# Vision tower kernel, one core: both image halves are loaded before the embedding matrix, and all patch strips are turned before the embedding begins

## The chip, the cores and the metric

One core of a Trainium2 chip runs the whole kernel in float32. The metric is the device time in microseconds (us), as the median of several executions. The profile is of one execution. Its engines are PE (TensorE matmul; PEld is its weight load), DVE (VectorE), ACT (ScalarE), POOL (GpSimd) and SP (SyncE, which here only issues transfers).

## The reference, cut to what matters

Sixteen images of 96 x 96 x 3 are cut into 6 x 6 patches of 16 x 16 x 3 = 768 values. Each patch is multiplied by a 768 x 192 matrix (the embedding), and attention and a soft mixture of 64 small MLPs follow.

```
h = einsum('bnk,kd->bnd', extract_patches(x, 16), W_proj) + b_proj + pos_emb   # 16 x 36 x 192
h = h + attention(layernorm(h))                    # 12 heads of 16, 36 tokens per image
h = h + soft_moe(layernorm(h))                     # 64 slots, fc1 192x768, gelu, fc2 768x192 each
```

The 64 pairs of fc1 and fc2 matrices are 75.5 MB of the 79.74 MB that the core moves. The change is in the first line alone.

## The kernel before

**Tiles.** There are 576 tokens. They are held in six row tiles `t` of three images (108 tokens), the last of one image (36 tokens). A patch's 768 values are six chunks of 128, which are the contraction of the embedding. Chunks 0 to 2 come from the upper eight pixel rows of each patch (`ph` = 0), chunks 3 to 5 from the lower eight (`ph` = 1).

**Images to chunks.** SP loads one half (`ph`) of all images with one DMA of 864 KB into `x_rows`: 96 partitions, one for each image and patch row, each 8 pixel rows long. Each half goes through the same steps:

1. `pixels` (L229) reorders the pixels so that each of the six patch columns `nw` is contiguous. DVE does columns 0 and 1 and then 2 and 3 (L633, two copies), ACT does columns 4 and 5 (L440, one copy).
2. PE turns each strip `n` = 6 ph + nw with three transposes of 96 x 128 (L907) into one of four PSUM banks (`n % 4`). It waits at L901 or L903 for the reordered pixels, and at L905 until the strip four before it has been copied out.
3. ACT copies the even strips to `patchesT` (L443), DVE the odd ones (L636). Both count them, in `x_kept_a` and `x_kept_d`, up to three for a half.

DVE and ACT work in program order, so the reordering of the second half stands behind the copies of the first half's strips on both engines.

**Embedding.** `embed(t, chunks)` (L877) issues one matmul per chunk (L881), with 192 columns out, into bank `4 + t % 4`. Tiles 0 to 3 keep their banks until their six chunks are summed, tiles 4 and 5 reuse banks 4 and 5. In the trace a float32 matmul or transpose is two records, so one strip of three transposes is six records and `embed(t, range(3))` is six records.

**Order on PE before the change.** Nine filler matmuls (`keep_busy`, L875, whose result nothing reads), then strips 0 to 5; two fillers; a wait for the matrix (`wp_in`) and for the six kept strips; `embed` of tiles 0 and 1 with chunks 0 to 2; strips 6 to 11; `embed` of tiles 2 and 3 with chunks 0 to 2; a wait for all twelve kept strips; and from L1092 on chunks 3 to 5 of tiles 0 to 2, the turning of the attention weights (`turn_weights`) between the rest of the embedding, and layer norm, attention and the routing.

**Order on SP.** First half of the images, embedding matrix, second half, three copies of the positional table, the biases and attention weights, and then the MLP's weights in units of 1536 KB (L270). The ring has room for 12 units. The last six slots overlap the buffers of the embedding and of the attention weights, so SP waits at L275 and L276 before it fills them. The other 36 units each wait at L281 until PE has used the unit in their slot, which first happens when the MLP begins. PE works through 48 units in eight groups of six.

```
x_in[ph]   -> DVE L633, ACT L440         (reordering)
wp_in      -> PE, ahead of the first embed
embedded   -> DVE L642 (adds the positional table, then layer norm), SP L275
```

Of the kernel before, what the change touches and what calls it, by code (L numbers as in the profile page):

```python
# [11 lines left out]
def vit_tower_kernel(nc, x, tok_w, tok_b, tok_pos, w_qkv, w_proj, attn_b, slots, slot_scale,  # L12
# [9 lines left out]


    B, IMG, _, CH = x.shape
    KP, D = tok_w.shape
    N = tok_pos.shape[0]
    GRID = 6
    PATCH = IMG // GRID
    NT = B * N
    HEADS, DH = 12, 16  # L30
    S, _, FF = fc1_w.shape
    EPS = 1e-5
    TPI = 3
# [23 lines left out]
    def rows(t):  # L57
        return min(TR, NT - TR * t)
# [4 lines left out]
    with ExitStack() as ctx:  # L63
# [3 lines left out]
        def sem(name):  # L67
            return ctx.enter_context(nc.semaphore(name))
# [101 lines left out]
        wqkv_in, wproj_in, wp_in = sem("wqkv_in"), sem("wproj_in"), sem("wp_in")  # L170
# [10 lines left out]
        x_turned, x_kept_a, x_kept_d = sem("x_turned"), sem("x_kept_a"), sem("x_kept_d")  # L181
# [60 lines left out]
        @block.sync  # L242
        def _(sp):
            for ph in range(2):
                sp.dma_start(x_rows[0:C2, ph, :],
                             x_view[:, ph * 8 * XR:(ph + 1) * 8 * XR]).then_inc(x_in[ph], 16)
                if ph == 0:
                    sp.dma_start(embed_w[:, :, :], tok_w.rearrange("(c p) d -> p c d", p=128)).then_inc(wp_in, 16)
            for j in range(TPI):
                sp.dma_start(pos_raw[j * N:(j + 1) * N, :], tok_pos).then_inc(pos_in, 16)  # L250
            sp.dma_start(pos_b[0:TR, :], tok_b.partition_broadcast(TR)).then_inc(pos_in, 16)
            sp.dma_start(qkv_raw[0:C2], w_qkv.rearrange("(t p) c -> p t c", p=C2)).then_inc(wqkv_in, 16)
            sp.dma_start(proj_raw[0:C2], w_proj.rearrange("(t p) c -> p t c", p=C2)).then_inc(wproj_in, 16)
            sp.dma_start(slot_rows[0:S, :], slots).then_inc(slots_in, 16)
            sp.dma_start(slot_sc[0:S, 1:2], slot_scale.rearrange("(s a) -> s a", a=1)).then_inc(slots_in, 16)
            sp.dma_start(b1_raw[0:S, :], fc1_b).then_inc(b1_in, 16)
            sp.dma_start(attn_b_row[0:TR, :], attn_b.partition_broadcast(TR)).then_inc(ab_in, 16)
            sp.dma_start(norm_row[0:TR, :], norm_w.partition_broadcast(TR)).then_inc(nw_in, 16)
            sp.dma_start(b2_rows[0:S, :], fc2_b).then_inc(b2_in, 16)

            def load_unit(g, slot):
                u = slot % UNITS
                if u < 3:
                    dst = ring[:, slot, :].rearrange("p (q o) -> p q o", q=GS // 2)
                    src = fc1_view[u][:, bass.ds(g * (GS // 2), GS // 2), :]
                else:
                    dst = ring[:, slot, :].rearrange("p (s n) -> p s n", s=GS)
                    src = fc2_view[:, bass.ds(g * GS, GS), 2 * (u - 3):2 * (u - 3) + 2, :].rearrange(
                        "p s c d -> p s (c d)")
                sp.dma_start(dst, src).then_inc(unit_in[slot], 16)  # L270

            for slot in range(RING):
                if slot == EARLY:

                    sp.wait_ge(embedded, TT)  # L275
                    sp.wait_ge(misc_turned, 2)  # L276
                load_unit(slot // UNITS, slot)
            with sp.Fori(1, GROUPS // 2) as it:
                for slot in range(RING):

                    sp.wait_ge(units_used, it * RING + (slot + 1 - RING))  # L281
                    load_unit(it * 2 + slot // UNITS, slot)
            for tt in range(3):
                sp.wait_ge(final_ready, (1, 2, 4)[tt])
                if tt < 2:
                    sp.dma_start(out_view[2 * tt * TR:2 * (tt + 1) * TR, :].rearrange("(t p) d -> p t d", p=TR),
                                 h[0:TR, 2 * tt:2 * tt + 2, :]).then_inc(out_written, 16)
                else:
                    for t in (TT - 2, TT - 1):
                        sp.dma_start(out_view[t * TR:t * TR + rows(t), :],  # L290
                                     h[0:rows(t), t, :]).then_inc(out_written, 16)
            sp.wait_ge(out_written, 64)
# [577 lines left out]
        def _(pe):  # L870
            def keep_busy(bank, count):


                for _ in range(count):
                    pe.matmul(ps[:, bank, 0:128], ident[:, :], ident[:, :], start=True, stop=True)  # L875

            def embed(t, chunks=range(KC)):  # L877
                if t >= 4:
                    pe.wait_ge(h_ready, t - 3)
                for c in chunks:  # L880
                    mm = pe.matmul(ps[0:rows(t), 4 + t % 4, 0:D], patchesT[:, c, t * TR:t * TR + rows(t)],  # L881
                                   embed_w[:, c, :], start=(c == 0), stop=(c == KC - 1))
                if chunks[-1] == KC - 1:
                    mm.then_inc(embedded, 1)
# [4 lines left out]
            for n in range(2 * GRID):  # L889
                if n == 6:  # L890

                    keep_busy(7, 2)
                    pe.wait_ge(wp_in, 16)
                    pe.wait_ge(x_kept_a, 3)
                    pe.wait_ge(x_kept_d, 3)
                    for t in range(2):
                        embed(t, range(3))
                ph, nw = n // 6, n % 6

                if nw < 4:  # L900
                    pe.wait_ge(regrouped_d, 2 * ph + nw // 2 + 1)  # L901
                else:
                    pe.wait_ge(regrouped_a, ph + 1)  # L903
                if n >= 4:
                    pe.wait_ge(x_kept_d if n % 2 else x_kept_a, (n - 4) // 2 + 1)  # L905
                for r in range(3):
                    mm = pe.transpose(ps[:, n % 4, r * C2:(r + 1) * C2],  # L907
                                      x_patch[0:C2, ph, nw, r * 128:(r + 1) * 128], ident[0:C2, 0:C2])
                mm.then_inc(x_turned, 1)

            embed(2, range(3))
            embed(3, range(3))
            pe.wait_ge(x_kept_a, 6)
            pe.wait_ge(x_kept_d, 6)

# [385 lines left out]
```

## Time and profile before

| | us |
|---|---|
| median of 3 runs | 247.25 |
| the three runs | 245.79, 247.25, 251.49 |
| span of the profiled execution, first to last instruction | 244.4 |
| PE busy in the span | 221.5 (91%) |
| DVE, ACT, POOL busy | 67.4, 64.0, 44.2 |
| data moved | 79.74 MB, mean 326 GB/s |

The profiled execution's own device time is not shown apart from its span; the median of the runs is 2.85 us above that span, the fastest run 1.39 us. The span is cut into 40 slices of 6.1 us on the page. The images, the strips and the embedding fill the first four or so, attention and routing go to about 85 us, and the MLP's eight groups take the rest. A busy share says only that an engine was at work: which wait ends last in a stretch is read from the chain and the timelines.

### The profile page before, as it was taken

To read this page: it belongs to the slowest core of one execution; us is meant where nothing else is said; L and a number is where in the kernel's file an instruction comes from. 1 tells how busy PE (TensorE), PEld (TensorE's weight loads), DVE (VectorE), ACT (ScalarE), POOL (GpSimd) and SP (SyncE) were. 2 spreads that over 40 slices of the span, in tenths; PEclk is the share of its full clock that TensorE was granted. 3 is DMA by queue.
4 is the path that set the end of the run, shared out by engine and by line. 5 is a ranking of instruction groups with operands and counts; after the bars stand their busy time and mean duration, and the time that the engine had idled before them with its cause. 6 is when DMAs were issued, how large, how long until landed. Compare 5 with 4: busy or idle time off the path is not lost.

```text
span 244.4 us, 5457 instructions
## 1 busy us (share of the span) xinstructions
PE 221.5 (91%) x2268; PEld 157.2 (64%) x2268; DVE 67.4 (28%) x166; ACT 64.0 (26%) x160; POOL 44.2 (18%) x80
## 2 busy tenths in 40 slices
PE   6799999999998889978979979997997999799794
PEld 6789756777767737635548547764664675576472
DVE  0557346678766532011011002002000200200202
ACT  2443242454656734021021021003002100300300
POOL 7501268663534020000000000001000000000000
PEclk9999999999999999997999997997699999999999
DMA  6999999999800059999999999999999999999952
GB/s 164 266 240 400 393 373 380 398 394 373 306 1 3 0 174 409 388 373 384 400 387 373 385 402 388 374 385 402 388 373 386 401 388 373 385 402 387 373 208 72
DMA packets 40904, 79.74 MB, mean 326 GB/s; under 512 B 1096, under 2 KB 28344, under 8 KB 40696
## 3 DMA queue, kind: packets, MB, share of 16 engines
q1 hardware_dynamic: 40888, 79.52, 90.8%
q8 instruction: 11, 0.18, 0.3%
q14 instruction: 5, 0.04, 0.0%
HBM read 79.07 MB, written 0.44 MB: 325 GB/s over the span
## 4 chain that ended last, share of the span: by engine, by line
PE 70%; DMA 9%; SPq 8%; ACT 5%; issue 3%; DVE 3%; POOL 1%; DVEq 0%; ACTq 0%
PE ps L1263 12%; PE ps L1223 11%; PE ps L875 10%; SPq L270 8%; DMA ring<-in_L_ffn_fc_weight_dram 6%; PE ps L1203 6%; PE ps L881 5%; PE ps L995 4%; PE ps L950 3%; DMA ring<-in_x_dram 3%; ACT region_p L593 2%; PE ps L968 2%; PE ps L1193 2%; PE ps L1239 2%; PE ps L907 2%
## 5 line engine op out<-in xcount | busy, mean ns | idle before, releaser
L875 PEld LDWEIGHTS ps<-ident 128*128 128x128 f32 x310 | 40.3, 208 | 10.6 <-issue 8.6
L875 PE MATMUL ps<-ident 128*128 128x128 f32 x310 | 44.9, 301 | 1.8 <-POOL neg_half L307 1.8
L846 DVE TENSOR_TENSOR region_p<-ps,b1T 128x384 f32<-128x384 f32 x16 | 8.2, 553 | 124.0 <-PE ps L1239 124.0
L1263 PE MATMUL ps<-ring,region_p 128*32 128x192 f32 x768 | 37.8, 352 | 1.2 <-ACT region_p L608 0.9
L1263 PEld LDWEIGHTS ps<-ring,region_p 128*32 128x32 f32 x768 | 24.9, 119 | 11.7 <-ACT region_p L608 2.7
L1223 PE MATMUL ps<-ring,qkvT 128*32 128x384 f32 x288 | 26.8, 490 | 0.0
L593 ACT COPY region_p<-ps 128x384 f32<-128x384 f32 x16 | 11.7, 831 | 55.3 <-PE ps L1223 55.3
L1203 PE MATMUL ps<-region_k,soft_space 128*108 128x192 f32 (+1 forms) x96 | 18.6, 336 | 0.4 <-ACT region_k L610 0.4
L1203 PEld LDWEIGHTS ps<-region_k,soft_space 128*108 128x108 f32 (+1 forms) x96 | 13.7, 163 | 7.1 <-issue 6.3
L429 POOL COPY qkvT<-region_k 128x384 f32 x6 | 3.1, 513 | 79.8 <-PE ps L1223 79.8
L1239 PE MATMUL ps<-ident,region_p 128*128 128x128 f32 x48 | 7.0, 282 | 11.4 <-ACT region_p L593 11.4
L610 ACT COPY region_k<-ps 128x192 f32<-128x192 f32 x8 | 2.5, 318 | 54.0 <-PE ps L1263 54.0
L352 POOL TENSOR_TENSOR region_k<-region_k,head_mask 96x432 f32<-96x432 f32 x16 | 14.3, 910 | 9.0 <-PE ps L968 6.8
L1239 PEld LDWEIGHTS ps<-ident,region_p 128*128 128x128 f32 x48 | 5.1, 141 | 16.3 <-ACT region_p L593 16.3
L1223 PEld LDWEIGHTS ps<-ring,qkvT 128*32 128x32 f32 x288 | 8.1, 109 | 9.9 <-issue 8.8
L881 PE MATMUL ps<-ring 128*108 128x192 f32 (+1 forms) x72 | 12.6, 328 | 0.1
L995 PE MATMUL ps<-qkvT,soft_space 96*108 96x192 f32 x64 | 11.8, 328 | 0.0
L608 ACT ACTIVATE region_p<-region_p 128x384 f32<-128x384 f32 x16 | 7.5, 514 | 15.4 <-DVE region_p L846 15.4
L881 PEld LDWEIGHTS ps<-ring 128*108 128x108 f32 (+1 forms) x72 | 10.8, 163 | 0.9 <-issue 0.2
L1193 PE MATMUL ps<-v_diag,region_k 64*128 64x288 f32 x32 | 10.5, 451 | 0.0
L995 PEld LDWEIGHTS ps<-qkvT,soft_space 96*108 96x108 f32 x64 | 10.2, 173 | 0.3 <-ACT soft_space L469 0.2
L1223 PE MATMUL ps<-ring,region_k 128*32 128x384 f32 x96 | 8.5, 489 | 0.6 <-DVE region_k L825 0.6
(137 smaller groups left out, 235.1 us busy)
## 6 DMA issues: line engine op xcount, KB each, us to landing
ring<-in_L_ffn_fc_weight_dram SPq DMA_DIRECT2D x48, 1536.0 KB, 15.9
ring<-in_x_dram SPq DMA_DIRECT2D x2, 864.0 KB, 8.8
ring<-in_L_tok_W_proj_dram SPq DMA_DIRECT2D x1, 576.0 KB, 7.7
ring<-in_L_attn_w_qkv_dram SPq DMA_DIRECT2D x1, 432.0 KB, 11.2
out_dram<-h SPq DMA_DIRECT2D x2, 162.0 KB
ring<-in_L_ffn_fc_bias_dram SPq DMA_DIRECT2D x1, 192.0 KB, 9.5
ring<-in_L_attn_w_proj_dram SPq DMA_DIRECT2D x1, 144.0 KB, 11.7
soft_space<-in_L_tok_pos_emb_dram SPq DMA_DIRECT2D x3, 27.0 KB
```

Source lines behind the costliest of these rows:

```text
L270: sp.dma_start(dst, src).then_inc(unit_in[slot], 16)
L352: pool.tensor_tensor(k_diag[0:C2, i % 2, og, :].rearrange("p (a h m) -> p a h m", a=2, h=HG), kT[0:C2, og, 2 * N * i:2 * N * (i + 1)].rear ...
L593: act.copy(hid[:, :, half * 64:(half + 1) * 64].rearrange("p c n -> p n c"), ps[:, half, 0:FF // 2].rearrange("p (n c) -> p n c", c=FC)).t ...
L846: dve.tensor_tensor(pre[:, 3 * half:3 * half + 3, :].rearrange("p c (s b) -> p c s b", s=GS), ps[:, 2 + half, 0:384].rearrange("p (c s b) ...
L875: pe.matmul(ps[:, bank, 0:128], ident[:, :], ident[:, :], start=True, stop=True)
L881: mm = pe.matmul(ps[0:rows(t), 4 + t % 4, 0:D], patchesT[:, c, t * TR:t * TR + rows(t)], embed_w[:, c, :], start=(c == 0), stop=(c == KC - 1))
L995: mm = pe.matmul(ps[0:TR, 2 + i % 2, a * D:(a + 1) * D], x_copies[0:C2, i % 2, c, a, :], qkvT[0:C2, c, 2 * D:3 * D], start=(c == 0), stop= ...
L1193: mm = pe.matmul(ps[:, half, 0:HALF], sel[0:S, gg, :], combT[0:S, half * HALF:(half + 1) * HALF], start=True, stop=True)
L1203: mm = pe.matmul(ps[0:r, 5 + t // 2, (t % 2) * D:(t % 2 + 1) * D], mix[:, gg, t * TR:t * TR + r], y2[:, gg, :], start=False, stop=False, s ...
L1223: mm = pe.matmul(ps[32 * q:32 * q + 32, half, 0:FF // 2], y, w[:, q, half * FF // 2:(half + 1) * FF // 2], start=(j == 0), stop=(j == 2), ...
L1239: mm = pe.transpose(ps[:, 2 + c // 3, (c % 3) * 128:(c % 3 + 1) * 128], hid[:, c, :], ident[:, :])
L1263: mm = pe.matmul(ps[32 * q:32 * q + 32, 4, 0:D], gact[:, 2 * u + cc, 2 * q + l, :], w[:, 2 * q + l, cc, :], start=first, stop=last, tile_p ...
```

## The change

SP issues the embedding matrix after the second half of the images. On PE the embedding of tiles 0 and 1 between the halves is gone; four filler matmuls stand there and no wait. After strip 11, PE waits for the matrix and for the first half's kept strips, and then runs chunks 0 to 2 of tiles 0 to 3 in one block.

```diff
             for ph in range(2):
                 sp.dma_start(x_rows[0:C2, ph, :],
                              x_view[:, ph * 8 * XR:(ph + 1) * 8 * XR]).then_inc(x_in[ph], 16)
-                if ph == 0:
+                if ph == 1:
                     sp.dma_start(embed_w[:, :, :], tok_w.rearrange("(c p) d -> p c d", p=128)).then_inc(wp_in, 16)
...
             for n in range(2 * GRID):
                 if n == 6:
 
-                    keep_busy(7, 2)
-                    pe.wait_ge(wp_in, 16)
-                    pe.wait_ge(x_kept_a, 3)
-                    pe.wait_ge(x_kept_d, 3)
-                    for t in range(2):
-                        embed(t, range(3))
+                    keep_busy(7, 4)
                 ph, nw = n // 6, n % 6
...
-            embed(2, range(3))
-            embed(3, range(3))
+            pe.wait_ge(wp_in, 16)
+            pe.wait_ge(x_kept_a, 3)
+            pe.wait_ge(x_kept_d, 3)
+            for t in range(4):
+                embed(t, range(3))
             pe.wait_ge(x_kept_a, 6)
             pe.wait_ge(x_kept_d, 6)
```

## Rows read from the trace of the kernel before

**Rows 1.** Page, 40 slices of the span: DMA busy share in tenths, and GB/s.

```profile
DMA  6999999999800059999999999999999999999952
GB/s 164 266 240 400 393 373 380 398 394 373 306 1 3 0 174 409 388 373 384 400 387 373 385 402 388 374 385 402 388 373 386 401 388 373 385 402 387 373 208 72
```

**Rows 2.** Busy time by stretch: PE, PEld, DVE, ACT, POOL, granted clock, DMA share, GB/s.

```profile
20.00:60.00 40.00, 39.25 (x324) 29.14 (x323) 25.00 (x67) 17.06 (x55) 21.33 (x31) 1.00 1.04 387
60.00:86.00 26.00, 24.01 (x255) 19.11 (x258) 17.19 (x52) 16.05 (x52) 9.26 (x14) 1.00 0.25 89
...
100.00:150.00 50.00, 44.28 (x479) 28.03 (x471) 5.24 (x9) 8.15 (x15) 2.37 (x6) 0.94 1.05 386
150.00:200.00 50.00, 46.80 (x543) 31.73 (x546) 3.50 (x6) 5.75 (x11) 1.58 (x4) 0.92 1.05 387
200.00:237.00 37.00, 33.76 (x376) 22.95 (x368) 3.44 (x6) 5.09 (x9) 0.00 (x0) 1.00 1.01 368
```

**Rows 3.** The chain that ended last, in time: start, us, what.

```profile
0.81 6.17 DMA ring<-in_x_dram
7.62 3.14 PE ps L907 x18
10.77 0.78 PE ps L875 x4
11.63 2.17 PE ps L881 x12
13.84 1.21 PE ps L907 x12
...
221.33 15.71 DMA ring<-in_L_ffn_fc_weight_dram
```

**Rows 4.** Timeline of DVE (first three rows) and ACT: start, us, instruction, idle before.

```profile
7.01 1.03 DVE L633 COPY ring<-ring 96x768 f32<-96x768 f32 x2 [7.01 <-DMA ring<-in_x_dram]
...
10.80 0.68 DVE L636 COPY ring<-ps 128x288 f32<-128x288 f32 x1 [0.28 <-PE ps L907]
13.23 1.02 DVE L633 COPY ring<-ring 96x768 f32<-96x768 f32 x2 [1.75 <-DMA ring<-in_x_dram]
...
10.32 0.67 ACT L443 COPY ring<-ps 128x288 f32<-128x288 f32 x1 [0.28 <-PE ps L907]
13.23 0.83 ACT L440 COPY ring<-ring 96x768 f32<-96x768 f32 x1 [2.23 <-DMA ring<-in_x_dram]
```

**Rows 5.** Timeline of PE: the fillers early and late, the second half's strips, the embedding.

```profile
1.76 4.21 PE L875 MATMUL ps<-ident 128*128 128x128 f32 x18 [1.76 <-POOL neg_half L307]
...
13.84 2.02 PE L907 MATMUL ps<-ident,ring 96*128 96x96 f32 x18
15.70 5.05 PE L881 MATMUL ps<-ring 128*108 128x192 f32 x30
...
79.64 1.60 PE L875 MATMUL ps<-ident 128*128 128x128 f32 x12
```

**Rows 6.** SP's issues: start and us of the issue.

```profile
0.81 0.41 SPq L245 DMA_DIRECT2D ring<-in_x_dram  x1
1.29 0.41 SPq L248 DMA_DIRECT2D ring<-in_L_tok_W_proj_dram  x1
1.75 0.53 SPq L245 DMA_DIRECT2D ring<-in_x_dram  x1
...
4.21 0.36 SPq L252 DMA_DIRECT2D ring<-in_L_attn_w_qkv_dram  x1
...
87.21 2.26 SPq L270 DMA_DIRECT2D ring<-in_L_ffn_fc_weight_dram  x2
```

**Rows 7.** Page, DMA issues: count, KB each, median us from issue to landing.

```profile
ring<-in_x_dram SPq DMA_DIRECT2D x2, 864.0 KB, 8.8
ring<-in_L_tok_W_proj_dram SPq DMA_DIRECT2D x1, 576.0 KB, 7.7
ring<-in_L_attn_w_qkv_dram SPq DMA_DIRECT2D x1, 432.0 KB, 11.2
```

## The prediction

> **What bounds the kernel now.** I read the slices of the page first, then the busy times by stretch, then the chain of waits over the first 20 us, and last the timelines of the engines there. In the slices, DMA is at nine tenths or more, near 390 GB/s, until about 61 us, nearly idle for the next three slices, and busy again to the end [rows 1]. The stretches say the same in numbers: a DMA share of 1.04 from 20 to 60 us, 0.25 from 60 to 86 us, and 1.05, 1.05 and 1.01 in the MLP [rows 2]. So there are two regimes. Up to the MLP PE sets the pace (39.25 of 40 us and 24.01 of 26 us busy), with the transfers ahead of it. From the first reload at 87.21 us [rows 6] the transfers set the pace, and the chain ends with 15.71 us of waiting for MLP weights [rows 3]. A reload waits until PE has used the unit in its slot. **A shift of the MLP's start therefore moves all 36 reloads and the end by the same amount**, and nothing in the MLP gives it back. The idle DMA between 61 and 80 us means that an earlier or later load of units in front of the MLP changes nothing.
>
> The changed stretch lies in PE's regime. The chain goes from the first image half (0.81 + 6.17 = 6.98 us) to strips 0 to 5 (7.62 to 10.76), fillers (to 11.55), the embedding of tiles 0 and 1 (11.63 to 13.80), and strips 6 to 11 from 13.84 [rows 3]. PE's gaps after 7.62 us are under 0.1 us each. So the removed embedding was not wasted time: it filled the wait for the second image half, whose reordering DVE and ACT begin at 13.23 us, after 1.75 and 2.23 us of idling for it [rows 4].
>
> **The transfers.** The landing times come from issue plus latency. First half: 6.98 us. Matrix: 1.29 + 7.7 = 8.99 us. The two halves average 8.8 us, so the second took 2 x 8.8 - 6.17 = 11.4 us from 1.75, which is 13.2 us [rows 6, 7] and agrees with DVE's start at 13.23. After the change the second half is issued at about 1.3 us, and the trace has no second-in-line transfer of that size. From both sides: at the pace at which the matrix landed behind the first half, 2.0 us for 576 KB, it lands 3.0 us after 6.98, at 10.0 us; at the pace of the second half behind the matrix, 4.2 us for 864 KB, at 11.2 us. I take 11, nearer to the row with its own size and row length. The matrix is then last of three with the same bytes in total, so I take 13.2 us. It could be as late as the attention matrix, three small tables further back in the queue: 4.21 + 11.2 = 15.4 us [rows 6, 7]. SP's three issues take 0.41, 0.41 and 0.53 us in either order, and the issues behind them don't move.
>
> **When strips 6 to 11 start.** Three things must be ready. DVE's reordering stands behind its copy of strip 5, which ends at 10.80 + 0.68 = 11.48 us [rows 4]; that is later than the landing, so DVE's order decides and not the transfer. From the start of the reordering to the first strip took 13.84 - 13.23 = 0.61 us: 12.09 us. The four extra filler records (two matmuls) cost 1.60/12 = 0.13 us each at the late rate or 4.21/18 = 0.23 us at the early one [rows 5], so the fillers end at 12.1 or 12.5 us. The first is free, hidden under DVE's reordering; the second costs 0.4 us. I take 12.09. ACT is free for its part at 10.99 us and needs 0.83 us [rows 4]: 11.8, earlier than DVE. **The strips move 1.75 us earlier.** They take 15.70 - 13.84 = 1.86 us [rows 5], which holds their waits for the copies by ACT and DVE, and end at 13.95 us.
>
> **The embedding.** Before, 12 records of chunks 0 to 2 were left at 15.70 us; at 5.05/30 = 0.168 us each [rows 5] they end at 17.72. After, 24 are left at 13.95: 4.04 us, to 17.99. The matrix (13.2) is there in time, the first half's strips were kept at 11.48, and the second half's are wanted only at 18. **Sum: 17.99 - 17.72 = +0.27 us.** In words: a block of 2.0 us was moved from before the strips to behind them; the strips move up by 1.75 us, because DVE isn't free any sooner. The rest of the program follows in the same order and shifts with it. DVE, which would have idled for the first summed tile in any case, has its copies done some 1.75 us sooner, and that is worth nothing. The profiled execution has a span of 244.4 us; with 2.85 us around it, which brings it to the median of the runs, the forecast is 247.5 us.
>
> **The clock.** The granted clock reads 1.00 over all rows up to 60 us [rows 2], that is the 2.4 GHz level, but durations differ: 18 records of strips took 3.14 us in the first half [rows 3] and 2.02 us in the second, and a filler 0.23 us early and 0.13 us late [rows 5]. I read the early ones as run at 1.2 GHz. The rise came while PE had worked without a pause from 7.62 us, nearly all of that on transposes.
>
> The Trainium skill, page "TensorE: Matmul & The Clock Gate", section "Part 4: PE-mode transpose", says that the full clock does not engage for transposes, since they don't count as PE being busy in the same way. By that rule the change would be harmful: it puts all strips close together, with only fillers between, and takes the ordinary matmuls out. This trace speaks against it, as the rise followed 3.14 us of transposes and 0.78 us of fillers.
>
> **Rivals.**
>
> *The second half lands no earlier* (the change doesn't do what it says). All three transfers are in flight together, so the order of issue may matter little. Then strips start at 13.84 as before, end at 15.70, and 24 records follow, to 19.74: +2.0 us, 249.3 us. PE idles some 1.7 us where it embedded before. It begins to cost when the half lands after 11.48 us, one for one. Against it: the matrix landed 4.2 us ahead of the half issued 0.46 us behind it, so order does count. Chance 0.10. This is my slower case.
>
> *The matrix is late.* PE then waits behind the strips, with everything queued behind. It decides from 13.95 us on; at 15.4 us it adds 1.5 us to the 0.27: 249.0 us. For it: the matrix has 768-byte rows and now shares the engines with small tables. Against it: the same bytes are ahead of it. Chance 0.10.
>
> *Strips 0 to 5 run at the full clock.* In an execution where the clock rises during the first fillers, they would take about 1.86 us instead of 3.14, and DVE would be free at about 10.2. The old kernel gains nothing from that, as it waits for the half until 13.2. The new one starts the second strips at 10.6 to 11.8 (landing plus 0.61) and ends them at 12.5 to 13.6; it embeds from 13.2 to 13.6 on and ends at 17.2 to 17.7: -0.5 to 0 us, 246.8 to 247.2 us. In the profiled execution it wasn't so. Chance 0.20.
>
> *The clock falls behind the strips.* If PE went back to 1.2 GHz for the block of 24 records, they would cost up to twice, +4.0 us: 251.5 us. This is what the rule of the skill's page would lead to. Against it: the pause ahead of the strips is 0.1 us or less. Chance 0.05.
>
> **How the numbers follow.** The forecast, +0.1 to +0.7 us, has 0.50. Beside the four rivals 0.05 is left for what the runs themselves do: the three before spread from 245.79 to 251.49, 2.3%, without any change. A median may well fall near the fastest, which gives the low end: 245.79 - 0.5, rounded down to 245.0. The high end takes in the first two rivals at 249.3 and half a microsecond of spread: 249.8. Only the fallen clock and spread lie outside. A difference of 2% is 4.9 us, about what a measurement of this kernel can tell from no change; no rival reaches it, so faster has 0.02, slower 0.04 and within 2% the rest.
>
> **What would show it.** Right: DVE's reordering of the second half starts at 11.48 us without idling for the transfer; first strip of the second half at about 12.1; an unbroken block of 24 embedding records from about 13.95; its end within 0.5 us of 17.7; the first reload near 87.5. Wrong: DVE or ACT idle for the images past 11.5 us (first rival), PE idle ahead of the block (second), embedding records over 0.2 us apart (clock). A change of more than 2 us at the first reload would make the sum wrong; one behind it, with the reload in place, would make the claim of the rigid shift wrong.

## The result, and the profile after

The changed kernel takes 247.78 us (median of 20 runs) against 246.72 us before (20 runs). The ratio is 1.0063 with a 95% interval of 1.0033 to 1.0093, which is a cost of 0.8 to 2.3 us: a small loss, but clear of zero. The ratio leaves slow executions out, and its cut falls unevenly here: six of the changed kernel's at 249.3 to 249.9 us are counted, five of the kernel before at 250.6 to 251.5 (and one at 1172.85) are not, and with those six left out too the ratio of the means would be 1.0031. The medians differ by 1.06 us. The forecast was 247.5 us, +0.27 us. In the profiled pair the span went from 244.4 to 245.7 us, and the first reload of an MLP unit from 87.21 to 88.40 us.

The chain of waits of the changed kernel over its first 22 us (start, us, what), which answers to [rows 3]:

```profile
0.82 6.54 DMA ring<-in_x_dram
...
7.38 0.57 DVE ring L633
...
7.99 3.14 PE ps L902 x18
11.13 1.76 PE ps L875 x8
12.89 2.19 PE ps L902 x18
15.09 6.84 PE ps L881 x42
```

PE does not pause from 7.99 us on, and the embedding is one block, as intended. Three terms differ from the sum. The first image half landed at 7.36 instead of 6.98 us. The fillers hold PE up to 12.89 us, against the 12.1 us at which the strips were forecast. And from the start of the second strips to the start of the embedding are 14.93 - 12.69 = 2.24 us in PE's timeline below, where 1.86 was taken over from before.

DVE, and under it ACT's reordering of the second half, in the changed kernel's timeline, against [rows 4]:

```profile
7.38 1.02 DVE L633 COPY ring<-ring 96x768 f32<-96x768 f32 x2 [7.38 <-DMA ring<-in_x_dram]
...
11.17 0.68 DVE L636 COPY ring<-ps 128x288 f32<-128x288 f32 x1 [0.29 <-PE ps L902]
11.69 1.01 DVE L633 COPY ring<-ring 96x768 f32<-96x768 f32 x2
13.82 1.98 DVE L636 COPY ring<-ps 128x288 f32<-128x288 f32 x3 [1.12 <-PE ps L902]
...
11.15 0.85 ACT L440 COPY ring<-ring 96x768 f32<-96x768 f32 x1
```

The second reordering follows the copy of strip 5 with no idle time for a transfer in its row. The prediction had this step, with the right releaser: the order of DVE's own program. DVE then waits 1.12 us for PE, which is still at its fillers.

PE's timeline and SP's issues (start, us), against [rows 5] and [rows 6], and the page's DMA rows (median us from issue to landing), against [rows 7]:

```profile
10.93 1.97 PE L875 MATMUL ps<-ident 128*128 128x128 f32 x8
12.69 2.40 PE L902 MATMUL ps<-ident,ring 96*128 96x96 f32 x18
14.93 7.00 PE L881 MATMUL ps<-ring 128*108 128x192 f32 x42
...
0.82 0.87 SPq L245 DMA_DIRECT2D ring<-in_x_dram  x2
1.73 0.42 SPq L248 DMA_DIRECT2D ring<-in_L_tok_W_proj_dram  x1
...
88.40 10.96 SPq L270 DMA_DIRECT2D ring<-in_L_ffn_fc_weight_dram  x4
...
ring<-in_x_dram SPq DMA_DIRECT2D x2, 864.0 KB, 7.8
ring<-in_L_tok_W_proj_dram SPq DMA_DIRECT2D x1, 576.0 KB, 10.7
```

The matrix lands at 1.73 + 10.7 = 12.4 us, ahead of the strips' end at 14.9. The two halves average 7.8 us and the first took 6.54, so the second took 9.1 us from about 1.27 and landed near 10.3. Both were needed later than that.

From the first reload to the end of the span are 157.2 us before and 157.3 us after. In this pair the MLP passes the shift on whole; its stretches have DMA shares of 1.05 and 1.05, as before [rows 2].

```profile
100.00:150.00 50.00, 44.25 (x530) 28.51 (x526) 5.19 (x9) 8.15 (x15) 2.38 (x6) 1.00 1.05 387
150.00:200.00 50.00, 46.83 (x528) 31.72 (x518) 3.56 (x6) 5.76 (x11) 1.58 (x4) 0.90 1.05 387
```

So the first reload of an MLP unit ("the reload" from here on) is a gauge of the front of the kernel that is free of what the long MLP adds. The experiments are read by it first, and then by their times.

### The profile page after: what moved, and what is told of

The parts are those of the page before. It is cut to its first block, busy times and chain, and to the rows that moved or that the text cites. A ratio compares the mean times of both kernels' runs of the same rounds, so it can differ in the third digit from the quotient of the medians.

```text
span 245.7 us, 5465 instructions
## 1 busy us (share of the span) xinstructions
PE 221.5 (90%) x2272; PEld 158.1 (64%) x2272; DVE 67.3 (27%) x166; ACT 64.0 (26%) x160; POOL 44.5 (18%) x80
## 4 chain that ended last, share of the span: by engine, by line
PE 61%; SPq 17%; DMA 9%; ACT 4%; issue 3%; DVE 3%; POOL 1%; DVEq 0%; ACTq 0%
SPq L270 17%; PE ps L1261 9%; PE ps L1221 9%; PE ps L875 8%; DMA ring<-in_L_ffn_fc_weight_dram 6%; PE ps L881 5%; PE ps L1201 5%; PE ps L993 4%; PE ps L948 3%; DMA ring<-in_x_dram 3%; PE ps L966 2%; PE ps L902 2%; ACT region_p L593 2%; PE ps L1237 2%; PE ps L1008 2%
## 5 line engine op out<-in xcount | busy, mean ns | idle before, releaser
L875 PEld LDWEIGHTS ps<-ident 128*128 128x128 f32 x314 | 41.2, 210 | 10.7 <-issue 8.7
L875 PE MATMUL ps<-ident 128*128 128x128 f32 x314 | 45.9, 302 | 1.8 <-POOL neg_half L307 1.8
L1261 PE MATMUL ps<-ring,region_p 128*32 128x192 f32 x768 | 36.5, 342 | 2.1 <-DMA ring<-in_L_ffn_fc_weight_dram 1.0
L1261 PEld LDWEIGHTS ps<-ring,region_p 128*32 128x32 f32 x768 | 24.2, 115 | 12.0 <-ACT region_p L608 2.7
L881 PE MATMUL ps<-ring 128*108 128x192 f32 (+1 forms) x72 | 12.4, 327 | 0.0
L993 PE MATMUL ps<-qkvT,soft_space 96*108 96x192 f32 x64 | 11.8, 328 | 0.0
L1191 PE MATMUL ps<-v_diag,region_k 64*128 64x288 f32 x32 | 10.7, 456 | 0.0
## 6 DMA issues: line engine op xcount, KB each, us to landing
ring<-in_L_tok_W_proj_dram SPq DMA_DIRECT2D x1, 576.0 KB, 10.7
```

Source lines behind the costliest of these rows:

```text
L993: mm = pe.matmul(ps[0:TR, 2 + i % 2, a * D:(a + 1) * D], x_copies[0:C2, i % 2, c, a, :], qkvT[0:C2, c, 2 * D:3 * D], start=(c == 0), stop= ...
L1191: mm = pe.matmul(ps[:, half, 0:HALF], sel[0:S, gg, :], combT[0:S, half * HALF:(half + 1) * HALF], start=True, stop=True)
L1261: mm = pe.matmul(ps[32 * q:32 * q + 32, 4, 0:D], gact[:, 2 * u + cc, 2 * q + l, :], w[:, 2 * q + l, cc, :], start=first, stop=last, tile_p ...
```

## The experiments

**Two fillers instead of four.**

```diff
-                    keep_busy(7, 4)
+                    keep_busy(7, 2)
```

> The changed kernel with two fillers between the halves instead of four, so the only edit is the added work. Theory A (the fillers are a term of the loss): strips 6 to 11 start when DVE's reordering is done, about 12.45 us instead of 12.69, and the first reload comes some 0.2 to 0.4 us before the changed kernel's 88.40; time 0.1 to 0.2% under the changed kernel. Theory B (the loss lies in the first landing and in the block that was moved): strips start within 0.1 us of 12.69, time as the changed kernel, ratio to before 1.005.

The ratio to before is 1.0025 (0.9973 to 1.0077). The first reload came at 88.60 us, later than in the changed kernel. PE's timeline, and the busy times by stretch (PE, PEld, DVE, ACT, POOL, granted clock, DMA share, GB/s):

```profile
7.72 2.02 PE L902 MATMUL ps<-ident,ring 96*128 96x96 f32 x18 [1.75 <-DVE ring L633]
9.57 1.05 PE L875 MATMUL ps<-ident 128*128 128x128 f32 x4
10.89 3.14 PE L902 MATMUL ps<-ident,ring 96*128 96x96 f32 x18 [0.27 <-DVE ring L633]
13.82 8.30 PE L881 MATMUL ps<-ring 128*108 128x192 f32 x42
...
8.00:10.00 2.00, 1.88 (x21) 1.72 (x19) 1.57 (x4) 1.70 (x3) 1.60 (x7) 0.91 0.92 238
10.00:12.00 2.00, 1.73 (x10) 1.44 (x10) 1.33 (x3) 1.37 (x3) 0.86 (x2) 0.50 1.11 299
12.00:14.00 2.00, 2.00 (x14) 2.00 (x13) 1.33 (x2) 1.43 (x3) 0.00 (x0) 0.50 1.13 251
14.00:16.00 2.00, 2.00 (x8) 1.90 (x7) 0.86 (x2) 0.26 (x1) 0.00 (x0) 0.50 1.06 174
```

Neither theory holds, and the interval of the ratio holds both. The second strips did start early, at 10.89 us, since the first ones ran fast (2.02 us). But then the granted clock was 0.50, the 1.2 GHz level, from about 10 to 16 us, and strips and embedding cost 3.14 and 8.30 us. Against the high level (2.02 and 7.00 us in a run below) that is 2.4 us, so the low level made this execution late. Whether the count of fillers had a part in the level is asked again further down.

**Only the transfers' order.**

```diff
-                if ph == 0:
+                if ph == 1:
```

(in the kernel before, all else unchanged)

> Only the transfers' order is changed: both halves first, then the matrix; PE's order is that of before. Theory A (the order of issue decides the landing): the second half lands near 10.4 us and the matrix near 12.5; PE idles in front of the embedding of tiles 0 and 1 until 12.5, so the second strips start at about 14.7 instead of 13.84 and the first reload is 0.8 to 1.2 us later than before: ratio 1.003 to 1.005. Theory B (the matrix would be there in time anyway): strips at 13.84, ratio 1.000. Both expect the first half to land at 7.0 to 7.4; if it is 0.3 us later than before, sharing the engines with the second half costs that.

The ratio is 1.0119 (1.0043 to 1.0194), the first reload 88.25 us. From its chain of waits:

```profile
1.73 11.10 DMA ring<-in_L_tok_W_proj_dram
...
12.88 2.20 PE ps L881 x12
15.08 0.99 PE ps L907 x12
```

Theory A by the trace: the matrix landed at 12.83 us and PE waited for it ahead of the embedding of tiles 0 and 1; the second strips began at 14.9. The ratio lies above theory A's 1.003 to 1.005, with an interval that reaches into it (six executions). The first half landed at about 7.6 us, later than either theory had it.

**Only PE's order** (the changed kernel with the transfers of before).

```diff
-                if ph == 1:
+                if ph == 0:
```

> Only PE's order is changed: four fillers, all strips, then the embedding; the matrix is still issued before the second half. This is the first rival of the prediction made real. Theory A (the embedding had filled the wait for the second half): the second half lands at 13.2, PE idles from about 12 to 13.84, the strips end at 15.7, and the block of 24 records ends at 19.7: first reload 2.0 us after before's 87.21, ratio 1.008. Theory B (the order of the block does not matter): ratio 1.000 to 1.003. If the clock also falls in the idle time, up to 4 us more.

The ratio is 1.0102 (1.0050 to 1.0154), the first reload 90.00 us. From the timelines of DVE and PE:

```profile
12.45 1.03 DVE L633 COPY ring<-ring 96x768 f32<-96x768 f32 x2 [1.01 <-DMA ring<-in_x_dram]
...
10.52 1.97 PE L875 MATMUL ps<-ident 128*128 128x128 f32 x8
13.06 3.14 PE L902 MATMUL ps<-ident,ring 96*128 96x96 f32 x18 [0.57 <-DVE ring L633]
```

This is the first rival made real, with DVE idle for the images as that rival said. The transfer was 0.8 us earlier here (12.45) than in the profile before (13.23), yet the reload came 2.8 us later. Of that 2.0 us is the block of 12 records that now stands behind the strips, as in theory A; the low level in the second strips (3.14 us) and at the start of the embedding (7.53 us for 42 records, against 7.00) outweighs the earlier landing and adds the rest. Neither half of the change is of use alone: both ratios are above the changed kernel's 1.0063, though the intervals overlap.

**A long warm-up in the changed kernel.**

```diff
-            keep_busy(7, 9)
+            keep_busy(7, 16)
```

> The changed kernel with 16 fillers instead of 9 at the very start, so that PE is busy without a pause up to the first strips. Theory A (the strips of the first half run at the low clock level, and the changed kernel, which no longer waits for the second half, can use the time): records of the first strips 0.08 us apart instead of 0.16, DVE free at about 10.3, second strips from about 11.0, embedding from 12.9, first reload about 86.5 (1.9 us before the changed kernel): ratio to before 0.996 to 0.999. Theory B (the first half's strips are paced by the copies of ACT and DVE, or the clock does not rise): second strips near 12.5 and ratio 1.003 to 1.006. A cost of up to 0.8 us if the fillers still run when the first strip is ready.

The ratio to before is 0.9996 (0.9953 to 1.0040), and the first reload 86.36 us, 2.0 us ahead of the changed kernel's. PE's timeline and two stretches:

```profile
7.85 2.02 PE L902 MATMUL ps<-ident,ring 96*128 96x96 f32 x18 [0.88 <-DVE ring L633]
9.71 1.08 PE L875 MATMUL ps<-ident 128*128 128x128 f32 x8
11.02 2.02 PE L902 MATMUL ps<-ident,ring 96*128 96x96 f32 x18 [0.23 <-DVE ring L633]
12.88 7.00 PE L881 MATMUL ps<-ring 128*108 128x192 f32 x42
...
8.00:10.00 2.00, 1.87 (x21) 1.72 (x21) 1.56 (x4) 1.60 (x4) 1.66 (x6) 1.00 0.89 222
10.00:12.00 2.00, 1.77 (x20) 1.58 (x18) 1.66 (x4) 1.65 (x3) 0.39 (x2) 1.00 1.11 316
```

Theory A in the trace, to 0.2 us in each step. With the clock high from the first strips on, both sets of strips take 2.02 us and eight filler records 1.08. The times show no loss any more, though the interval still has room for one of 0.4%.

**The same warm-up in the kernel before** (the same edit).

> The kernel before, with 16 fillers at the start instead of 9. Theory A (the clock of the first 20 us sets the sum, but the old order waits for the second half in any case): the clock stays high, the first strips end at about 9.9 us, yet the second ones still start at 13.8 and the first reload comes at 87.1 to 87.3 as before; ratio 0.998 to 1.000, and the long warm-up's gain in the changed kernel (2.0 us at the first reload) belongs to the two changes together. Theory B (the gain is the warm-up's own): first reload near 86.4 and ratio 0.995.

The ratio is 0.9991 (0.9949 to 1.0033), the first reload 86.10 us, so theory B's position at the reload; its ratio of 0.995 is only just inside the interval. The part of theory A that failed was its fixed transfer. The second half was ready for DVE at 12.12 us, 1.1 us earlier than in the first profile:

```profile
12.12 1.02 DVE L633 COPY ring<-ring 96x768 f32<-96x768 f32 x2 [1.97 <-DMA ring<-in_x_dram]
```

The old order did wait for it (1.97 us idle on DVE), and all of its gain against 87.21 is that earlier landing. With the clock high in both, the changed order is 0.26 us behind the old one at the reload (86.36 and 86.10).

**Four tiles embedded between the halves**, with the old order and 16 fillers.

```diff
-                    for t in range(2):
+                    for t in range(4):
                         embed(t, range(3))
...
-            embed(2, range(3))
-            embed(3, range(3))
```

> The kernel before with 16 fillers at the start and all four tiles embedded with chunks 0 to 2 between the halves, so the wait for the second half is filled with 24 records instead of 12. Theory A (PE is the bound whenever it doesn't wait): embedding from about 10.7 to 14.6, second strips to 16.5, first reload about 1.2 us before before's 87.21, and 0.3 us before the changed kernel with the long warm-up (86.36): 86.0; ratio 0.994 to 0.997. Theory B (the order of strips and embedding does not matter once the clock is high): same as that kernel, 86.4.

A miss: first reload 87.09 us, ratio 1.0039 (0.9999 to 1.0079). PE's timeline:

```profile
10.69 4.12 PE L881 MATMUL ps<-ring 128*108 128x192 f32 x24 [0.38 <-DVE ring L636]
14.64 1.96 PE L907 MATMUL ps<-ident,ring 96*128 96x96 f32 x18
17.46 3.15 PE L881 MATMUL ps<-ring 128*108 128x192 f32 x18 [0.85 <-DVE ring L636]
```

The wait for the second half was filled, but chunks 3 to 5 now came straight behind the strips and waited 0.85 us for DVE's copies of the last ones. The embedding that used to stand behind the strips had covered these copies. And the 16 fillers ran until 8.0 us, past the first half's landing at 6.8.

**The changed kernel again**, no edit.

> The changed kernel once more, unedited. Theory A (the point at which the clock rises is drawn anew in each execution and is a part of the loss): the rise comes at another time than 13.59 us, the strips of the one or the other half run at the other level, and the first reload lies between 87.4 and 89.5. Theory B (the clock rises a fixed time after PE's work): rise at 13.6 within 0.1 and first reload at 88.4. In both the first half lands at 7.1 to 7.6. Ratio 1.004 to 1.008.

The ratio is 1.0054 (1.0016 to 1.0092). This confirms the loss. The first reload came at 87.19 us, 1.2 us earlier than in the first profile of the same kernel. PE and the clock:

```profile
7.69 2.16 PE L902 MATMUL ps<-ident,ring 96*128 96x96 f32 x18 [1.72 <-DVE ring L633]
9.64 1.96 PE L875 MATMUL ps<-ident 128*128 128x128 f32 x8
11.40 2.47 PE L902 MATMUL ps<-ident,ring 96*128 96x96 f32 x18
13.71 7.00 PE L881 MATMUL ps<-ring 128*108 128x192 f32 x42
...
10.00:12.00 2.00, 2.00 (x12) 2.00 (x12) 1.42 (x3) 1.01 (x2) 0.41 (x2) 0.50 1.10 305
12.00:14.00 2.00, 2.00 (x18) 1.92 (x17) 1.39 (x3) 1.62 (x3) 0.00 (x0) 0.79 1.18 251
```

Here the first strips ran at the high level (2.16 us) and the fillers at the low one (1.96 us). In the first profile the first strips were slow too. So the level of each piece differs from execution to execution, as theory A had it, but the reload fell 0.2 us below theory A's bounds.

**The kernel before again**, no edit.

> The kernel before once more, unedited, for its profile. Theory A: the first clock record lies elsewhere than 11.28 us, and the first reload is 87.2 within 0.3 all the same, because the second strips wait for a transfer and not for the clock. Theory B: rise at 11.3 and reload at 87.2. In both the first half lands at 6.9 to 7.1, earlier than with the second half right behind it.

One execution, 247.46 us; first reload 86.69 us, 0.5 us earlier than in the first profile. DVE's second start:

```profile
12.60 1.02 DVE L633 COPY ring<-ring 96x768 f32<-96x768 f32 x2 [1.64 <-DMA ring<-in_x_dram]
```

The second half landed at 12.6 instead of 13.2 us, and that moved the reload more than theory A allowed. Against this execution the changed kernel's second one is 0.50 us later at the reload, against 1.19 us in the first pair.

**Three tiles between the halves, 14 fillers**, old order.

```diff
-            keep_busy(7, 9)
+            keep_busy(7, 14)
...
-                    for t in range(2):
+                    for t in range(3):
                         embed(t, range(3))
...
-            embed(2, range(3))
             embed(3, range(3))
```

> The kernel before with 14 fillers at the start and three tiles embedded between the halves; the fourth stays behind the last strips, where it covers the copies of strips 10 and 11. Theory A (PE is the bound, the clock stays high, and the copies are covered): 18 records from about 10.3 to 13.3, second strips from 13.3 to 13.9, first reload 85.6 to 86.3, under the old order with the long warm-up (86.10) or equal to it; no idle time over 0.3 us ahead of chunks 3 to 5; ratio 0.993 to 0.998. Theory B (the wait for the second half decides): as that kernel, 86.1, ratio 0.999.

First reload 86.05 us, inside theory A's bounds, and its 18 records end at 13.8, half a microsecond later than theory A had them. But theory B had 86.1 and 0.999, and the ratio is 0.9992 (0.9944 to 1.0041). The run doesn't tell the two apart, and there is no gain that can be told from none.

**The same with nine fillers.**

> The same with the nine fillers of before. Theory A (the third tile fills what is left of the wait; the clock comes on top): first reload 0 to 0.4 us before before's two profiles (86.69 and 87.21), ratio 0.997 to 1.000. Theory B (only the clock matters): ratio 1.000, first reload 86.7 to 87.2.

First reload 86.91 us, ratio 1.0011 (0.9977 to 1.0045): between before's two profiles, so theory B. The second half landed at 12.3 us, and six more records between the halves (11.49 to 14.6) then only delayed the strips.

**Two fillers, again.**

> The changed kernel with two fillers between the halves, a second look. Theory A (with fewer fillers PE idles 0.2 to 0.3 us ahead of the second strips, and where that idle time falls in a stretch at the low level, the level stays low for some microseconds longer): if the clock is low when the first strips end, there is idle time ahead of the second strips only if the first strips ran at the high level; if the first strips run at the low level throughout, fillers end at about 11.9 and strips start at 12.1 to 12.5, with the first reload at 87.5 to 88.0. Theory B: first reload at 88.6 in any case.

One execution, 248.59 us; first reload 88.21 us. PE:

```profile
7.50 2.54 PE L902 MATMUL ps<-ident,ring 96*128 96x96 f32 x18 [1.88 <-DVE ring L633]
9.83 1.11 PE L875 MATMUL ps<-ident 128*128 128x128 f32 x4
11.19 3.14 PE L902 MATMUL ps<-ident,ring 96*128 96x96 f32 x18 [0.25 <-DVE ring L633]
```

Again PE idled for 0.25 us ahead of the second strips with the clock low (0.50 from 10 to 14 us), and they took 3.14 us. Together with the first execution: in both, an idle of a quarter of a microsecond stood in the low stretch, and the reload came at 88.2 to 88.6. The unedited kernel whose clock had also fallen during the first strips (the repeat above) had four fillers and no idle, and reached 87.19. In two executions with PE's order of before (the kernel before again, and only the transfers' order) the level fell during the first strips too, PE had no idle time in the low stretch, and the granted clock was 1.00 again from 12 us on. That fits theory A, on five executions and by position alone; the times do not confirm it.

**The changed kernel with 14 fillers at the start.**

> The changed kernel with 14 fillers at the start. Theory A (the changed order loses only some 0.3 us to the old one once the clock stays high): first reload 86.2 to 86.8, ratio 0.999 to 1.002, and 0.2 to 0.8 us above the kernel with three tiles between and 14 fillers. Theory B (the changed order needs 16): clock low in a part of the strips, first reload over 87.

Ratio 1.0008 (0.9962 to 1.0054), first reload 86.95 us, just outside theory A's bounds and inside its ratio. The clock stayed high. What was late was the first half: 

```profile
7.84 1.02 DVE L633 COPY ring<-ring 96x768 f32<-96x768 f32 x2 [7.84 <-DMA ring<-in_x_dram]
```

That is 0.63 us after the 7.21 of the kernel with 16 fillers, whose reload came 0.59 us earlier. Between these two executions the first landing goes through to the reload nearly one for one.

## Why the prediction was right

The forecast had the way of the change, the unbroken block and its place in the range right. Its size was too small: +0.27 us was forecast, and 1.06 us (medians) and 1.19 us (the reload) were measured. That 247.5 lies so near 247.78 is luck. The prediction put 2.85 us around the span, from the median of three executions; the changed kernel's profiled execution took 247.42 us with a span of 245.7, so 1.7 us. This error of 1.1 us made up for the missing part of the loss. Of the signs that it named, DVE's start without a wait (11.69 us) and the unbroken block came, while the strips (12.69 against 12.1), the block's start (14.93 against 13.95) and the reload (88.40 against 87.5) were all late.

**The bound and the rigid shift.** Right for the profiled pair, and not in every execution. From the first reload to the end of the span were 157.2 to 157.8 us in eleven of the fourteen profiled executions and 158.6 to 159.0 in the other three, with reloads from 86.05 to 90.00 us. Nothing gave a shift of the front back. In the three longer ones (only PE's order, the kernel before again, two fillers again), and in the first one with two fillers, the chain that ended last has no transfer behind 100 us: PE's own work set the pace there. In the other ten it ends with a transfer of MLP weights, as in [rows 3]. The same matmuls in the two profiles of the kernel before (the first profile first, granted clock 1.00 and 0.50 there), and two late pieces of the second one's chain:

```profile
192.83 2.81 PE L1263 MATMUL ps<-ring,region_p 128*32 128x192 f32 x64
...
192.43 4.51 PE L1263 MATMUL ps<-ring,region_p 128*32 128x192 f32 x64
...
236.06 2.21 PE ps L875 x18
238.27 1.48 PE ps L1263 x32
```

So PE is close behind the transfers in the MLP, and a low clock there can make an execution 1 to 2 us longer whatever its front does. That is argued from these rows and not tested: the mean granted clock from the reload on was 0.95 in the three, but also 0.95 in the first profile of the kernel before.

**What the moved block had covered.** Right, and shown from both sides: only the transfers moved, PE waited for the matrix (reload +1.04 us); only PE's order moved, PE waited for the images (+2.8 us, in which the low clock has a part).

**When the strips start.** The gate was named rightly, DVE's own order. Its time was off because the working took the first landing as fixed at 6.98 us. Over the seven profiled executions with the matrix second in line, DVE's first reordering started at 6.58 to 7.01 us, 6.89 in the mean; over the seven with the second half second, at 6.89 to 7.84, 7.31 in the mean. That is +0.42 us, with single executions that overlap, and the new order passes it on, as it no longer waits for the second half. In the first pair it was +0.37 us, of which 0.16 came back because DVE began the reordering at 11.69 us, before its copy's row ends at 11.85. The prediction had said that the issues behind don't move, and had not asked what the transfer behind does to the one ahead of it. Why a half behind it delays the first half more than the matrix does, no run shows.

**The fillers.** Mis-sized. Of its two prices, free under the reordering at the late rate or +0.4 us at the early one, I took the first. All eight records ran at the early rate in both profiles of the changed kernel (1.97 and 1.96 us), and with the clock high they took 1.08 us. The upper price was the right one.

**The strips.** 1.86 us was taken from a stretch at the high level. In the changed kernel the strips come 1.15 us earlier, and part of them ran at the low level: 14.93 - 12.69 = 2.24 us, +0.38.

**The sum again.** To the +0.27 come +0.21 for the start of DVE's reordering (11.69 against 11.48), +0.39 for the fillers (12.69 against 11.69 + 0.61), and +0.38 for the strips: 1.25 us, against 1.19 us measured at the reload. With the clock held high the orders differ by 86.36 - 86.10 = 0.26 us, but in that pair the first half's landings also differ by 0.6 us, so the agreement with +0.27 is partly luck. The loss is two things: the first landing, and work that was moved into a stretch where the clock may still be low. A kernel that waits for a transfer hides a slow start; one that doesn't wait pays for it. That warming up first brings the ratio from 1.0063 to 0.9996 and 1.0008 fits this, though the intervals of these runs reach to 1.004 and 1.005 and so overlap with the changed kernel's.

The Trainium skill's page "TensorE: Matmul & The Clock Gate", section "What's actually happening", says that the moment of the rise varies between runs of the same kernel. The traces agree: two profiles of each kernel had the first strips once at 3.14 us and once at 2.63 (before) or 2.16 us (changed).

**The rivals.** The second half did land earlier (near 10.3 us) and the matrix was in time (12.4), so neither transfer rival came true. The full clock in the first strips did occur, in the repeat, and the strips then started at 11.40 us, inside the 10.6 to 11.8 given; but the clock then fell, and its reload was 0.02 us ahead of the first profile of the kernel before and 0.50 us behind the second, so the gain forecast for that case did not come. A low level in the block, the last rival, came only in part and in kernels where PE had idled ahead of the strips: the 42 records took 8.30 us with two fillers, against 7.00. Through transposes, as the Trainium skill's page "TensorE: Matmul & The Clock Gate", section "Part 4: PE-mode transpose", would have it, it is not borne out: in the warmed-up kernels the level stayed high through both sets of strips. No row shows, though, whether these transposes run in the mode that the Trainium skill's page speaks of. In the five executions in which it fell, PE had paused for 1.72 us or more ahead of the first strips; with 14 or 16 fillers the pause was 1.36 us at most, and it did not fall. In the remaining four, the first profiles of both kernels among them, the first strips took 3.14 us, so the level had not yet risen. That the length of the pause decides is argued from this order alone. The low level outlasted the pause by microseconds.

**Open.** The medians' loss of 1.06 us lies between the two pairs of profiles (0.50 and 1.19 us at the reload); the ratio's 1.55 us (0.63% of 246.72) lies above both. The changed kernel's executions at 249.3 to 249.9 us lift the ratio, and none of them was profiled, so what makes them longer, and whether the change has a part in it, is open.

## What to carry to other kernels

Before moving work out of a wait, ask what the wait was hiding: a slow clock and the jitter of a landing cost nothing while an engine waits for a transfer anyway, and both come to the surface once it doesn't. Which transfer is issued right behind the first one can move the first one's landing (here by 0.42 us in the mean). And work that stands behind a producer may be covering the copies of its last results; moving all of it forward uncovers them, as the four tiles between the halves did.

## What was unexpected of the hardware

A low clock level can begin well after the pause that it follows. After a pause of 1.75 us ahead of the first strips, the strips ran at the high level (2.02 us); then the granted clock fell while PE was at work, to 0.50 over the stretches from 10 to 16 us in one execution. A pause of 0.25 us in that low stretch went with a return of the level 2 to 5 us later than without it (two executions against three).

The same 864 KB transfer, issued third at about 1.75 us, was ready for DVE between 12.12 and 13.23 us in seven executions of the old order. One profile's landing is good to about half a microsecond, more than the whole term that was being argued about.
